# Splitting two local layers into parts of a woven pipeline and giving all engines a new order of steps

## What is computed

```
x = layernorm(x + self_attention(x))            # 16 heads, queries = keys = x, values x @ W_h
x = layernorm(x + cross_attention(x, context))  # 16 heads of 8, window |i - j| <= 64
y = x
for l in range(2):                              # two local layers
    h = shift_token(y)                          # half of the channels one token later
    q, k, v = split(h @ wqkv[l])                # 8 heads of 64
    q, k = rotary(l2norm(q) * qs), rotary(l2norm(k) * ks)
    y = y + softmax(q @ k.T, windowed) @ v @ wo[l]
    h = layernorm(shift_token(y)) * lg + lb
    a, g = split(h @ w1[l] + b1[l])
    y = y + (a * gelu(g)) @ w2[l] + b2[l]
out = layernorm(x + y)
```

## Time and profile before

| | |
|---|---|
| median of 3 runs | 1535.69 us (1531.51 to 1535.7) |
| the profiled execution | 1535.67 us |
| its span, first to last instruction | 1533.9 us |
| granted TensorE clock, mean | 0.959 |
| DMA | 8 GB/s over the span, nearly all of the weights at the start |

### The profile page before, as it was taken

One profiled execution on the slowest core, in us unless ns is written; L12 is line 12 of the kernel. 1 busy time (PEld: TensorE's weight loads), 2 busy tenths in 40 slices (PEclk: granted clock), 3 DMA queues, 4 the chain that ended last, 5 costly groups with the idle time before them and its releaser, 6 DMA issues. The chain is left out here.

```text
span 1533.9 us, 38526 instructions
## 1 busy us (share of the span) xinstructions
PE 1377.0 (90%) x11993; PEld 938.6 (61%) x12088; DVE 1004.8 (66%) x2900; ACT 952.5 (62%) x2562; POOL 880.1 (57%) x1289
## 2 busy tenths in 40 slices
PE   4778999999999999999999999999999999998764
PEld 2445666666666666666666666666666666666553
DVE  1446677676677776766776767767767677677432
ACT  1234666676666766766667667666676676666642
POOL 1034556666665567666655676666555766665533
PEclk8678999999999999999999999999999999999975
DMA  4000000000000000000000000000000000000000
GB/s 146 11 5 4 5 7 5 5 2 5 5 5 5 5 3 5 2 5 5 5 5 5 3 5 2 5 5 5 5 5 3 5 2 5 5 4 4 3 3 4
DMA packets 21645, 12.47 MB, mean 8 GB/s; under 512 B 5816, under 2 KB 20834, under 8 KB 21474
## 3 DMA queue, kind: packets, MB, share of 16 engines
q1 hardware_dynamic: 21600, 11.95, 2.6%
HBM read 9.84 MB, written 2.10 MB: 8 GB/s over the span
## 5 line engine op out<-in xcount | busy, mean ns | idle before, releaser
L787 ACT ACTIVATE local_e<-local_ps,local_bias,local_rn 128x128 f32<-128x128 f32 x512 | 229.0, 491 | 18.1 <-DVE local_bias L961 18.0
L1109 POOL TENSOR_TENSOR local_rn<-local_sc,half_neg 128x8 f32<-128x8 f32 x128 | 212.7, 1662 | 7.5
L1127 POOL TENSOR_TENSOR local_e<-local_e,local_rd 128x512 f32<-128x512 f32 x128 | 133.0, 1040 | 134.5 <-DVE local_rd L965 133.3
L956 DVE TENSOR_REDUCE local_m<-local_ps 128x4 f32<-128x512 f32 x128 | 88.6, 692 | 104.6 <-PE local_ps L648 104.6
L569 PE MATMUL self_ps<-self_z,self_e 128*128 128x129 f32 x1024 | 147.5, 288 | 1.7 <-DVE self_y L890 0.8
L890 DVE SCALAR_TENSOR_TENSOR self_y<-self_ps,self_rd,self_y 128x128 f32<-128x128 f32 x448 | 133.2, 345 | 9.2
L569 PEld LDWEIGHTS self_ps<-self_z,self_e 128*128 128x128 f32 x1024 | 129.0, 197 | 15.8 <-issue 7.8
L1026 POOL TENSOR_SCALAR local_x<-local_out 128x256 f32<-128x256 f32 x32 | 12.9, 404 | 216.3 <-issue 216.3
L942 DVE TENSOR_TENSOR local_cosp<-local_ps,cos_t 128x512 f32<-128x512 f32 x128 | 87.2, 682 | 71.7 <-ACT local_sq L770 71.7
L556 PE MATMUL self_ps<-wz,self_kT 128*128 128x512 f32 x256 | 128.4, 626 | 1.8 <-ACT self_kT L732 1.8
L787 ACT ACTIVATION_READ_ACCUMULATOR local_e<-local_ps,local_bias,local_rn 128x1 f32 x512 | 122.4, 239 | 0.0
(11 more groups left out here) (173 smaller groups left out, 3436.1 us busy)
## 6 DMA issues: line engine op xcount, KB each, us to landing
self_xin<-x SPq DMA_DIRECT2D x32, 64.0 KB, 1.7
cross_cin<-ctx_in SPq DMA_DIRECT2D x32, 64.0 KB, 1.8
out<-local_out SPq DMA_DIRECT2D x32, 64.0 KB, 1.6
wqkv_s<-wqkv SPq DMA_DIRECT2D x2, 768.0 KB
wz<-w_heads SPq DMA_DIRECT2D x1, 1024.0 KB, 5.6
w_r<-w SPq DMA_DIRECT2D x2, 341.0 KB
con<-consts SPq DMA_DIRECT2D x1, 644.0 KB, 3.6
wo_s<-wo SPq DMA_DIRECT2D x2, 256.0 KB
```

What stands on the lines that cost most here:

```text
L787: nc.scalar.activation(s.e[:, a, p, :], bank[:, 128 * p:128 * p + 128], ACT.Exp, bias=s.bias[:, a, p:p + 1], scale=s.rq[:, a, p:p + 1], ac ...
L956: nc.vector.tensor_reduce(s.m[:, a, :], bank.rearrange("p (c t) -> p c t", c=LH // 2), AX.X, ALU.max, negate=True)\
L1109: nc.gpsimd.tensor_tensor(s.rn[:, heads], s.sc[:, heads], half_neg[:, 0:LH], ALU.pow).then_inc(done, 8)
L1127: nc.gpsimd.tensor_tensor(s.e[:, a, :, :], s.e[:, a, :, :], s.rd[:, a, :].unsqueeze(2).to_broadcast([128, LH // 2, 128]), ALU.mult)\
```

## The change

Each local part is cut in two at a step boundary, on all engines: the local attention behind the turned keys (L637) into A and D (first layer) and B and E (second), the MLP behind the turned norm (L684) into M and O (first) and N and P (second). The code of the steps is the same. A table `SKEW` sets the iteration of each part: M, the first MLP's head, now runs at i-3 like its local attention, one iteration earlier than before; O stays at i-4, all others stay too. The four order strings are new throughout. New letters mean the same step in the same iteration as before except for those of M.

```diff
+LETTERS = ("ADMO", "BENP")
+SKEW = {"S": 1, "C": 2, "A": 3, "D": 3, "M": 3, "O": 4, "B": 4, "E": 4, "N": 5, "P": 5}
...
 ORDER_TENSOR = (
-    "MANAANMNMANMNMCSCBSSBCCSSBCCSABCACSCAASBBCSCBBSCSSCSASBCASSBABAB")
+    "AONOAANOPPBSABPBCSCSBSASACCSDDCCBBSECECSCSCCSCCSSDDSCSDSSDEEMEME")
...
                 for l in range(2):
-                    if at(i, 3 + l) is not None:
-                        parts["AB"[l]] = local_attention(l, at(i, 3 + l))
-                    if at(i, 4 + l) is not None:
-                        parts["MN"[l]] = local_mlp(l, at(i, 4 + l))
+                    for letter, part in zip(LETTERS[l], (attention_head, attention_tail, mlp_head, mlp_tail)):
+                        v = at(i, SKEW[letter])
+                        if v is not None:
+                            parts[letter] = part(l, v)
                 weave(order, parts)
...
-            def local_attention(l, v):
+            def attention_head(l, v):
...
                 last.then_inc(s.kT_psum, STEP)
                 yield
+
+            def attention_tail(l, v):
+                s = LOC[l]
                 pe.wait_ge(s.qT_ready, v + STEP)
...
-            def local_mlp(l, v):
+            def mlp_head(l, v):
...
                 nc.tensor.transpose(s.m1[:, 0:128], s.hn[:, :], ident).then_inc(s.hT_psum, STEP)
                 yield
+
+            def mlp_tail(l, v):
+                s = LOC[l]
                 pe.wait_ge(s.hT_ready, v + STEP)
```

More of the change, by code:

```diff
@@ L405, in decoder_kernel, with stages @@
         N_PREP_P = 5
-        def stages(eng, order, prepare_local, self_stage, cross_stage, local_attention, local_mlp):
+        def stages(eng, order, prepare_local, self_stage, cross_stage, attention_head, attention_tail, mlp_head, mlp_tail):
             def iteration(i):
                 parts = {}
-                if at(i, 1) is not None:
-                    parts["S"] = self_stage(at(i, 1))
-                if at(i, 2) is not None:
-                    parts["C"] = cross_stage(at(i, 2))
+                if at(i, SKEW["S"]) is not None:
+                    parts["S"] = self_stage(at(i, SKEW["S"]))
+                if at(i, SKEW["C"]) is not None:
+                    parts["C"] = cross_stage(at(i, SKEW["C"]))
                 for l in range(2):
-                    if at(i, 3 + l) is not None:
-                        parts["AB"[l]] = local_attention(l, at(i, 3 + l))
-                    if at(i, 4 + l) is not None:
-                        parts["MN"[l]] = local_mlp(l, at(i, 4 + l))
+                    for letter, part in zip(LETTERS[l], (attention_head, attention_tail, mlp_head, mlp_tail)):
+                        v = at(i, SKEW[letter])
+                        if v is not None:
+                            parts[letter] = part(l, v)
                 weave(order, parts)
```

20 lines of the change are left out of this document (10 added, 10 removed).

## The result

The changed kernel takes 1537.56 us (median of 11 executions, 1530.9 to 1543.43) against 1532.11 us for the one before (11 executions, 1530.51 to 1535.7): ratio 1.0034, 95% interval 1.0018 to 1.0050. The forecast was 1534, 2 us under the 1535.69 that three executions had given for the kernel before. Over 11 executions that kernel has 1532.11, so the change I forecast was -2 us and the measured one is +5.4, to the slower side by a little more than the 0.3% within which I had most of the forecast's weight. The profiled execution took 1539.45 us with a span of 1537.7.

What follows compares the result with a forecast made beforehand. TensorE was taken as the bound, busy 90% of the span. Start -2.55, middle +0.6 and end +1.9, with a walk through the order, gave +0.3 per period: 1535.7 + 8 - 10 = 1534 us, range 1509 to 1558.

Steps and rivals of the forecast that it cites:

- Start: Iteration start: TensorE's waits around both MLPs fall from 3.4 to 0.85 us, a gain of 2.55 us per period.
- Middle: Mid-iteration: waits, mainly for exponentials behind the first local attention's, grow from 0.8 to 1.4 us, a loss of 0.6.
- end: Iteration end: the second local attention alone exposes hand-over waits, 2.0 us against 0.1 before, a loss of 1.9.
- The 0.3 for the last single self product: Iteration end: 0.3 us wait for the eighth to twelfth head sums on VectorE behind the cross residual.
- The terms of the first: Iteration end, second local attention's transposes and evictions: hand-overs less TensorE's covering work, given as 0.75 us of wait.
- The period: One full iteration: 44.0 us, +0.3, giving +8 us over 28 full iterations.
- Filling and draining: First and last iterations: -10 us in all, between -4 and -16, from the drain's shorter starts.
- The drain's first two terms: Drain: 5.3 us won in the iteration starting at 1478.11, 3 in the one ahead of it.
- The third: Drain, the earliest of its three counted iterations: 2 us won by the shorter start.
- The table drain: Rival, ScalarE's table load before the first MLP's gate: extra drain puts L700 at +5.7, 1570 us; chance 0.02.
- The clock: Rival, waits at iteration end and start: granted clock falls each period, costing 1 us per period, 1562 us; chance 0.03.
- The other two: Rivals: middle and end covered, 1513 us, chance 0.29; serial end costs more through late attention weights, 1551 us, chance 0.26.

Runs made afterwards that it cites:

- e11: Changed kernel without GpSimd's two steps in the first MLP's norm (VectorE multiplies by the variance, other output), VectorE's order kept: 1536.44 us, ratio to before 1.0019.
- e5: Changed kernel, meant to alter ScalarE's order in iteration 33 alone, but both strings were identical, so the same program again: 1536.02 us, ratio to before 1.0035.
- e9: e8 plus ten unneeded matmuls in the changed kernel's iteration 33, six ahead of L479 and four ahead of L597: 1531.30 us, ratio to before 0.9991.
- c1: The kernel before with samples 16 to 31 left out, half the samples: 830.92 us.
- c2: The changed kernel with samples 16 to 31 left out, half the samples: 833.63 us.
- e7: Changed kernel without GpSimd's two steps in the first MLP's norm, fourth head step right behind the third on VectorE: 1547.99 us, ratio to before 1.0102.
- e6: Changed kernel with only the first sample's first-MLP head moved from the end of iteration 3 to the start of iteration 4: 1539.98 us.
- e8: Changed kernel with seven unneeded matmuls in TensorE's waits of iteration 3: 1533.42 us, ratio to before 1.0011.
- e10: Kernel before with six unneeded matmuls in iteration 3, two ahead of L522 and four ahead of L493: 1528.34 us, ratio to before 0.9977.
- e3: Kernel before with its order of steps, only the first MLP's head moved to the end of the iteration before: 1671.73 us, one execution.

## Why the forecast was wrong

- **Start (-2.55).** Right: 0.38 before L708, no wait before L697, the second local attention at +6.38 (6.4 by the forecast). That the waits come out a little smaller than 0.85 answers to the period's 0.1.
- **Middle (+0.6) and end (+1.9).** Right in places, and in sizes within 0.3: 0.42 and 0.25 for cross exponentials, where I had 0.6 and 0.15, 0.34 for GpSimd's keys (0.2), 0.47 and 0.94 at the end (0.75 and 0.9). The 0.3 for the last single self product did not come. (The terms of the first add up to 0.82, not 0.75: 0.69 + 0.69 + 0.07 - 0.43 - 0.2.) What I named as the releaser of the 0.94, the chain over GpSimd, is only one of several that tie; e11 shows VectorE's queue ahead of it.
- **The period (+0.3).** Measured +0.21 (+0.19 in e5's execution), +5.9 or +5.2 instead of +8. Right.
- **Filling and draining (-10). This is the step that failed.** The profiled pair has -5.4 in the drain and +3.25 in the fill, together -2.1. The drain's first two terms are right in that pair: from iteration 34's start to the last L618 are 45.6 us instead of 53.7, of which 5.4 and 2.8 in iterations 35 and 34, where I had 5.3 and 3. The third, 2 us won in iteration 33, is 2.7 us lost: the cross exponentials wait behind the first local attention's, TensorE stands 1.63 and 1.23 us, and the clock falls. e9's fillers take 2.6 of the 2.7 away, but the stretch behind is longer in that execution, and the whole drain is then 6.2 us shorter than before's, not 10. So the three terms don't simply add up, and the fall in iteration 33 is the smaller part of what is missing. To the fill I gave no term. Where the clock stays up it costs nothing (178.77 to iteration 5's mark in e5 against 178.97 in c1), but in the profiled pair it costs 3.25: behind its wait of 1.5 us in iteration 3 the changed kernel loses 6.7 us, and the kernel before loses 4.2 in its own fill against c1.
- **Rivals.** The table drain: L708 starts 4.3 us after the iteration's start, where the row gave 4.4. By the Trainium skill's rule (ScalarE: Activation LUTs, section "What ACT_TABLE_LOAD costs") it would have been 5.7; the trace does not agree. *The clock* was asked about the ends of the iteration, and a fall in each period did not come: in the changed kernel's two profiles (e5's is the second) it stays at 1.00 in full iterations behind waits of 0.94. It fell in fill and drain, and in the profiles of c2 and e7 once in a full iteration. The other two did not come.

In e5's execution, where the clock stays up in the fill, the terms make +5.2 - 5.5 - 0.2, no change to speak of, which is what the shortest executions of both show (1530.9 and 1530.5). The 5.4 us between the medians go with the clock: the record has each execution's mean granted clock, 0.966 and 0.967 for the changed kernel's two short ones, 0.956 to 0.960 for the five from 1539.4 up, and 0.962 to 0.965 for the four between, of which the two at 1536.5 and 1536.8 have 0.965, hardly less than the short ones. Where the clock fell is known for profiled executions alone. That TensorE's idleness makes the fill's fall is supported and not shown: of four profiles with the same fill and no fillers up to there (the changed kernel's, c2's, e5's, e6's) two have the fall and two don't, and e8's alone proves nothing; the times speak for it, with 14 of 21 at 1536.5 or above without fillers, 4 of 12 in e8 and 1 of 12 in e9. One rival is untested: falls in full iterations, as in c2's iteration 10 (+4.5 us), can make long executions too, and no run put fillers there.

## What to carry to other kernels

Moving a head into the previous iteration moved the waits with it, since several chains ended there together; before such a move, list all queues that end at the new place, not the one that is moved. Where a gain is to come from fill and drain, read the granted clock of those stretches, in more than one execution if there are: behind a wait of 1.5 us there one execution lost 6.7 us against another. A handful of matmuls that no one needs, put into the waits, was a cheap remedy here (e10: six of them, 0.23% below the kernel before; e9: seventeen, 0.4% below the changed kernel). And before a run is read as an answer, see in its trace that the order it was to change is another one: e5's was not.

## What the runs showed of the hardware

- The same program with the same waits was granted the full clock in one execution and half of it for 13.7 us in another, behind a wait of 1.5 us in iteration 3. In full iterations it stayed behind waits of 0.94 us in both profiles of the changed kernel, but fell once behind one of 0.42 in c2 (iteration of 48.4 us instead of 43.9) and once in e7 (47.2 instead of 44.3). Behind one of 2.71 us it fell in each iteration (e3).
- VectorE's norm of a 128x128 tile takes 0.35 us alone, 1.18 where GpSimd's 128x512 product ran (761.28 to 762.32; the norm, begun at 761.23, ended at 762.41), and 0.62 beside GpSimd's 128x128 addition (742.22 in the changed kernel). The Trainium skill (SBUF — State Buffer, section "SBUF: two separate sides") says that the two engines take turns at a pair of ports for a whole instruction; both rows, whose norms end 0.09 and 0.08 us behind GpSimd's instruction, agree. It also says that the one that starts first has the pair; by the start times of the records the norms were first, by 0.05 and 0.08 us, so that part is not borne out here.
